# Row maxima of attention scores: one head's piece per bank, or whole banks that hold several heads

## The reference, cut to what matters

```python
qkv = clip(einsum('bsd,ed->bse', xn, Wqkv), -8, 8)
q, k = layer_norm(q), layer_norm(k)            # with weights and biases
scores = einsum('bqhd,bkhd->bhqk', q, k) * 16**-0.5 + slopes * (k_pos - q_pos)
scores = where(k_pos <= q_pos, scores, -1e30)
out = einsum('bhqk,bkhd->bqhd', softmax(scores), v) @ Wout.T
x + out * silu(ffn(xn))
```

## Time and profile before

| | us |
|---|---|
| median of 3 runs (lowest, highest) | 1176.12 (1174.08, 1177.57) |
| profiled execution, its own time | 1172.21 |
| its span, first to last instruction | 1170.4 |
| PE busy in the span | 1090.4 (93%) |
| DVE busy | 905.7 (77%) |
| ACT busy | 632.1 (54%) |
| POOL busy | 374.2 (32%) |

### The profile page before, as it was taken

One profiled execution on the slowest core, in us unless ns is written; L12 is line 12 of the kernel. 1 busy time (PEld: TensorE's weight loads), 2 busy tenths in 40 slices (PEclk: granted clock), 3 DMA queues, 4 the chain that ended last, 5 costly groups with the idle time before them and its releaser, 6 DMA issues. The chain is left out here.

```text
span 1170.4 us, 23869 instructions
## 1 busy us (share of the span) xinstructions
PE 1090.4 (93%) x6401; PEld 679.4 (58%) x6401; DVE 905.7 (77%) x2115; ACT 632.1 (54%) x956; POOL 374.2 (32%) x472
## 2 busy tenths in 40 slices
PE   6999996999999999999999998899999999999996
PEld 4778771333333333333333433688788878887885
DVE  6888888788788888878888883677857876777776
ACT  3333330666667667666667667644544464445443
POOL 2666662121221212121221212134523443443343
PEclk9999995999999999999999999999999999999999
DMA  6335373334543434344443522100110020012000
GB/s 239 111 106 159 114 196 93 119 116 103 149 105 90 134 89 129 90 125 103 124 120 91 132 73 85 37 1 10 55 45 0 18 90 0 0 36 73 1 1 37
DMA packets 99725, 99.34 MB, mean 85 GB/s; under 512 B 28144, under 2 KB 80992, under 8 KB 99552
## 3 DMA queue, kind: packets, MB, share of 16 engines
q1 hardware_dynamic: 73216, 85.82, 25.4%
q10 hardware_dynamic: 26464, 12.98, 3.7%
HBM read 77.13 MB, written 21.23 MB: 84 GB/s over the span
## 5 line engine op out<-in xcount | busy, mean ns | idle before, releaser
L878 ACT ACTIVATE pr<-pair 128x1024 f32<-128x1024 f32 (+3 forms) x384 | 292.1, 811 | 157.9 <-PE pair L1001 101.4
L273 DVE CUSTOM_DVE_ANT_0 bank<-bank,sg 128x384 f32<-128x384 f32 (+3 forms) x512 | 241.5, 515 | 74.8 <-PE bank L283 70.4
L1281 DVE SCALAR_TENSOR_TENSOR gate<-pair,sgu,gate 128x512 f32<-128x512 f32 x168 | 126.1, 751 | 95.3 <-PE pair L1365 95.2
L1364 PE MATMUL pair<-xc_lo,w_gu 128*128 128x512 f32 x448 | 175.6, 392 | 1.8 <-DVE xc_lo L1264 1.8
L1365 PE MATMUL pair<-xc_hi,w_gu 128*128 128x512 f32 x448 | 174.8, 390 | 0.0
L276 DVE TENSOR_REDUCE mx<-bank 128x1 f32<-128x512 f32 x256 | 159.8, 682 | 7.4 <-PE bank L283 6.7
L1135 POOL TENSOR_TENSOR h_lo<-gate,h_hi 128x512 fp32r<-128x512 f32 x56 | 72.5, 1294 | 245.4 <-ACT h_hi L1160 245.4
L283 PE MATMUL bank<-xin_c,s_sb 108*128 108x512 bf16 (+3 forms) x384 | 116.7, 349 | 13.1 <-DVE mx L273 10.2
L1195 ACT ACTIVATE gate<-gate 128x512 f32<-128x512 f32 x56 | 35.5, 634 | 169.6 <-DVE gate L1281 169.6
L283 PE MATMUL bank<-ks,qs 108*128 108x512 bf16 (+3 forms) x384 | 109.0, 330 | 7.9 <-DVE mx L273 6.9
L996 PE MATMUL pair<-s_sb,xin_c 111*128 111x512 bf16 (+3 forms) x384 | 94.6, 330 | 8.8 <-DMA s_sb<-dt 4.1
(11 more groups left out here) (111 smaller groups left out, 1968.4 us busy)
## 6 DMA issues: line engine op xcount, KB each, us to landing
stk<-parts ACTq DMA_DIRECT2D x16, 768.0 KB, 5.0
zst<-in_z_all SPq DMA_DIRECT2D x24, 448.0 KB, 4.2
xin_c<-in_x SPq DMA_DIRECT2D x32, 256.0 KB, 2.7
sst<-in_w_all SPq DMA_DIRECT2D x16, 448.0 KB, 5.1
s_sb<-stk SPq DMA_DIRECT2D x96, 64.0 KB
xin_c<-stk SPq DMA_DIRECT2D x96, 64.0 KB
qs<-stk SPq DMA_DIRECT2D x96, 64.0 KB
ks<-stk SPq DMA_DIRECT2D x96, 64.0 KB
```

The source lines that it names most:

```text
L273: dve.tensor_tensor_reduce(out=src, in0=src, in1=tri[:, 512 - w:512], scale=1.0, scalar=-3.0e38, op0=ALU.add, op1=ALU.max, accum_out=dst). ...
L878: act.activation(pr[e % 3][:, 2 * p:2 * p + 2, 0:w], pair[p][:, :, 0:w], ACT.Exp, scale=SCALE)\
L1281: dve.scalar_tensor_tensor(out=a, in0=GB[j % 4], scalar=scale_of(n, k, it), in1=a, op0=ALU.mult, op1=ALU.add)\
L1364: pe.matmul(GB[j % 4], w, xc_lo[:, k, :], start=True, stop=False)
```

## The change

1. **Pieces of whole banks.** The diagonal block of a query tile is a piece of its own: all 4 heads, 128 keys each, in one bank. The keys left of the diagonal are cut at 512; a remainder of 128 keys takes 4 heads to a bank, one of 256 keys 2 heads, one of 384 keys 1. A group has 38 pieces (27 early, 11 late) in place of 48 (32 and 16), with 72 score matmuls in place of 48.
2. **Masks by matmul.** Into each of the 8 diagonal banks a first matmul (`behind` against the identity, repeated 4 times, 512 columns) writes the mask; the four score matmuls add to it. `take` is then always one `tensor_reduce` with one maximum per head of the bank. `tri` goes.
3. **Negation on VectorE.** `negate` replaces `over_halves`: a `tensor_reduce` with `negate=True` over the parts of each maximum (2 for tiles 0 to 3, 3 for tiles 4 to 7; the tiles are set to -3e38 once), twice a group. GpSimd's `chain` loses its first operation, 4 are left. The wait of VectorE for `d_chain` moves from the first piece of each kind to `negate`.
4. **D0 counts two turns** of the ring (`D0_TURNS`), so that the ring's length is divisible by 3: the piece behind `D0` waits until the piece ahead of `D0` is taken.
5. **Spread by number.** Places are weighted by how long TensorE's steps last (`steps_of`), and every piece counts one. `HEAD`, `TAIL` and `BEFORE` go from 8, 6, 4 to 5, 3, 2.
6. Small tiles (maxima, negated maxima, `behind`) move into `sg0`; `behind` is loaded once, in the first block in place of `tri`, no longer on SyncE's queue at the start of the second.

```diff
-        tri = sg0
-        mx0 = sb("mx0", [P, GH, 4], F32)
-        mx1 = sb("mx1", [P, 2, GH, 4], F32)
+        mx0 = sg0[:, 0:32].rearrange("p (a t j) -> p a t j", a=2, t=4)
+        mx1 = sg0[:, 32:80].rearrange("p (a t j) -> p a t j", a=3, t=4)
+        dneg0, dneg1 = sg0[:, 80:96], sg0[:, 96:112]
+        behind = sg0[:, 128:192].bitcast(BF16)
...
+        def pieces(qt):
+
+            out = [(qt, qt * P, P, 0, GH)]
+            for k0 in range(0, qt * P, 512):
+                w = min(512, qt * P - k0)
+                n = 1 if w > 256 else 512 // w
+                out += [(qt, k0, w, j0, n) for j0 in range(0, GH, n)]
+            return out
...
+        EARLY = sorted(sum((pieces(qt) for qt in range(4, 8)), []), key=lambda pc: pc[1] == 0)
+        LATE = sum((pieces(qt) for qt in range(4)), [])
+        HEAD = 5
+        LATER_KEYS = sum(pc[1] > 0 for pc in EARLY)
...
-        TAIL = 6
-        BEFORE = 4
+        TAIL = 3
+        BEFORE = 2
+        D0_TURNS = 2
...
-            width = [w for e in range(NSTEP) for w in (512 - STEPS[e][2], 512 - STEPS[e][2], 512 - STEPS[e - 1][2])]
-            total, work = sum(width[lo:hi]), sum(pc[3] + 60 for pc in lot)
+            def steps_of(e):
+
+                w = 512 - STEPS[e][2]
+                second_w, pv_w = 2 * w + (2 * P if diag[e] else 0), 4 * w + 384
+                return second_w, pv_w
+            width = [w for e in range(NSTEP) for w in (steps_of(e)[0], steps_of(e)[0], steps_of(e - 1)[1])]
...
-                while at < len(lot) and (h == hi - 1 or sum(pc[3] + 60 for pc in lot[:at]) < work * passed / total):
+                while at < len(lot) and at * total < len(lot) * passed:
...
-        RING = len(order)
+        RING = len(order) - 1 + D0_TURNS
...
+            dve.tensor_reduce(dst, b[:, 0:heads * w].rearrange("p (j c) -> p j c", c=w), AX.X, ALU.max).then_inc(m_free, 1)
...
+            mask = k0 == qt * P
+            if mask:
+
+                pe.matmul(b[:, :], behind, identb[:, :].unsqueeze(1).to_broadcast([P, GH, P]), start=True, stop=False)
+            for j in range(heads):
+                mm = pe.matmul(b[:, j * w:(j + 1) * w], qs[s][0:ROWS_MAX, qt // 4, j0 + j, (qt % 4) * P:(qt % 4 + 1) * P],
+                               ks[s][0:ROWS_MAX, j0 + j, k0:k0 + w], start=not mask, stop=not mask or j == heads - 1)
...
-        def over_halves(dve, n):
+        def negate(dve, n, mx, dneg, done):
 
             dve.wait_ge(m_free, n)
-            dve.tensor_tensor(mx1[:, 0, :, :], mx1[:, 0, :, :], mx1[:, 1, :, :], ALU.max).then_inc(mx1_done, 1)
+            dve.tensor_reduce(dneg.rearrange("p (j t) -> p j t", j=GH), mx.rearrange("p c t j -> p j t c"),
+                              AX.X, ALU.max, negate=True).then_inc(done, 1)
```

More of the change, by code:

```diff
@@ L193, in load @@
                   .then_inc(stk_in[s][b], 16)
-        m_full, m_free, mx1_done, tri_done = sem("m_full"), sem("m_free"), sem("mx1_done"), sem("tri_done")
+        m_full, m_free, mx_set = sem("m_full"), sem("m_free"), sem("mx_set")
+        neg0_done, neg1_done, behind_in_sb = sem("neg0_done"), sem("neg1_done"), sem("behind_in_sb")
         b_m, b_o = bank[0:3], bank[3]
@@ L203, in build, with columns @@
         diag = [kt >= 4 * qb for qb, kt, _ in STEPS]
[L206 to L216, removed]
+        def pieces(qt):
[5 more added lines that the diff above has]
+            return out
+        def columns(pc):
+            return pc[2] * pc[4] * (2 if pc[1] == pc[0] * P else 1)
+        EARLY = sorted(sum((pieces(qt) for qt in range(4, 8)), []), key=lambda pc: pc[1] == 0)
+        LATE = sum((pieces(qt) for qt in range(4)), [])
+        HEAD = 5
+        LATER_KEYS = sum(pc[1] > 0 for pc in EARLY)
         PLACES = 3 * NSTEP
@@ L250, in build, with numbered @@
         PREP = len(HEAD_ORDER)
-        number = ({x: n for n, x in enumerate(order)}, {x: n for n, x in enumerate(own)})
+        def numbered(work):
+            return {x: n + (D0_TURNS - 1 if "D0" in work[:n] else 0) for n, x in enumerate(work)}
+        number = (numbered(order), numbered(own))
         def at(x, last):
@@ L359, in body @@
                         if first and u == 1:
-                            sp.dma_start(tri[:, :], tri_in).then_inc(tri_done, 16)
+                            sp.dma_start(behind, behind_in).then_inc(behind_in_sb, 16)
                             sp.dma_start(raw_out[:, :, :], wproj[:, :, 3 * D:].rearrange("k p c -> p k c"))\
@@ L645, in _ @@
                     take(dve, EARLY[n], b_m[n % 3], n)
[L646 removed]
+                negate(dve, len(EARLY), mx1, dneg1, neg1_done)
             @block.tensor
@@ L939, in ring @@
                         elif x in LATE[HEAD:] or not last:
-                            if x == EARLY[0]:
-                                dve.wait_ge(d_chain, 10 * i + 1)
-                            if x == LATE[0]:
-                                dve.wait_ge(d_chain, 10 * i + 6)
                             take(dve, x, ring_bank(x, last), base(i) + at(x, last))
                             if x == EARLY[-1]:
-                                over_halves(dve, base(i) + at(x, last) + 1)
+                                dve.wait_ge(d_chain, 2 * CH * i + CH)
+                                negate(dve, base(i) + at(x, last) + 1, mx1, dneg1, neg1_done)
+                            if x == LATE[-1]:
+                                dve.wait_ge(d_chain, 2 * CH * i + CH)
+                                negate(dve, base(i) + at(x, last) + 1, mx0, dneg0, neg0_done)
                 dve.memset(b_o[:, :], 0.0).then_inc(o_clear, 1)
@@ L1000, in second @@
                         for jj in range(2):
-                            mm = pe.matmul(pair[p][:, jj, 0:P], identb[:, :], behind[:, :], start=False, stop=True)
+                            mm = pe.matmul(pair[p][:, jj, 0:P], identb[:, :], behind, start=False, stop=True)
                     mm.then_inc(s_full[p], 1)
```

70 lines of the change are left out of this document (29 added, 41 removed).

## The result

| | before | after |
|---|---|---|
| median (lowest, highest), us | 1175.68 (1174.08, 1177.57), 4 runs | **1188.7** (1186.53, 1189.56), 4 runs |
| profiled execution's span, us | 1170.4 | 1184.6 |
| PE / DVE busy, us | 1090.4 / 905.7 | 1106.5 / 872.9 |

The ratio is 1.0107, 95% interval 1.0086 to 1.0129: slower by 13 us, almost four times what a measurement can tell from no change. The forecast was 1177.9 (no change); the range, up to 1190, holds the time.

The account below looks back on a forecast made before the run. The prediction took TensorE in the attention loop (busy 93.57 of 100 us) as the bound. Its terms summed to +0.12 us a group, x 15 = +1.8 us on a median of 1176.1, giving 1177.9 us; the range was 1166 to 1190.

Parts of the forecast that it names:

- steps 1 and 2: Attention group: one bank for five small pieces in step 2, -0.49 us; narrower late pieces of query tile 3, -0.16.
- step 3: Attention group: TensorE's work there gives 3.23 us in place of 3.31, -0.08 a group, bounds -0.4 and +0.3.
- steps 4 and 5: Attention group, ahead of D0's turn: no change expected, 0; step 5 keeps the same 512-wide pieces.
- step 6, D0's double turn: Attention group: the next piece's matmul starts 0.5 us late, until VectorE begins D0's copy; taken as +0.40, bounds 0 and 0.85.
- steps 7 and 8: Attention group: same 512-wide pieces; one moves from step 8 to step 7, +0.21 and -0.21 us, together 0.
- steps 9 and 10: Attention group: a 0.055 us matmul ahead of a `pv` becomes a 0.43 us bank, twice, with no wait to absorb it: +0.75.
- step 11: Attention group's end: two banks (0.75 us) replace four pieces with a wait for a bank (1.05 us): -0.30.
- the reading of step 2: Five small pieces' 1.45 us come from handing three banks to and fro; rival, TensorE's issue: 1192 us, chance 0.07.
- the rival with 1200 us: Packed banks: weight loads don't hide, scores cost 0.096 us in place of 0.055, 22 us in all; chance 0.06.
- The rival's threshold of 0.51: Slower rival on D0's double turn, chance 0.18: decides from a D0 term of 0.51 us, where the sum passes 0.23 a group.
- The edges: First block's end and `negate`, GpSimd and queue changes: `negate` and queues at nothing, both edges together 0, bounds -2 and +2 us.
- D0 at VectorE's bound: Steps 6 to 9: D0's wait paid on TensorE and again by VectorE, term 0.85 us a group, 1184.7 us; chance 0.18.

Follow-up runs that it names:

- mask_twice: The changed kernel with each mask matmul issued a second time into the same bank: 1210.39 us, ratio 1.0304.
- o0_turn: The changed kernel with D0 counting one turn of the ring and the normalising entry O0 at the group's end two: 1183.78 us, ratio 1.0076.
- pad48: The changed kernel with an unused tile of 48 floats a partition, putting the first block's tiles back at their addresses before the change: 1180.52 us, ratio 1.0050.
- before_pad16: The kernel before with one unused tile of 16 floats (64 bytes a partition) ahead of `mx0`: 1181.7 us, ratio 1.0067.
- pad48_o0_turn: The changed kernel with the edits of both pad48 and o0_turn: 1175.11 us, ratio 1.0003.
- merged: pad48_o0_turn with one bank moved behind the last `pv` and step 10's packed bank moved behind D1's transpose: 1163.65 us, ratio 0.9907.
- pad16: The changed kernel with an unused tile of 16 floats, so that the projections' tiles start 128 past a multiple of 256 bytes: 1184.41 us, ratio 1.0088.
- align_xin_only: The changed kernel padded so that among the projections' tiles only `xin` starts at a multiple of 256 bytes, `parts` and `vst` 64 past: 1188.51 us, ratio 1.0127.

## Why the prediction was right and wrong

By its own steps, in us per group:

| step of the prediction | forecast | measured |
|---|---|---|
| steps 1 and 2: one bank for five pieces; narrower pieces | -0.65 | -0.63 |
| step 3 | -0.08 | +0.08 |
| steps 4 and 5 | 0 | +0.02 |
| step 6, D0's double turn | +0.40 | +0.55 |
| steps 7 and 8 | 0 | +0.02 |
| steps 9 and 10 | +0.75 | +0.75 |
| step 11 | -0.30 | -0.28 |
| sum | +0.12 | +0.51 |
| outside the sum, in the whole loop: three odd groups wait for D1's DMA | 0 | +1.5 us |
| outside the sum, in the whole loop: group 0 grew by less than the others | 0 | -0.4 us |
| outside the loop: the projections | 0 | +5.1 us |

- **Right**: the reading of step 2 (the ring's hand-overs, not TensorE's issue), the packed scores at 0.055 to 0.056 apart, eight in a row (so the loads do hide in a row as short as that, and the rival with 1200 us is dead), packed maxima at 0.60, and steps 9 to 11. mask_twice shows the path that the sum assumed.
- **D0, mis-sized.** "I take +0.40, as some 0.1 of idle lies ahead of the next `pv`". The wait was 0.56 and all of it was paid: o0_turn takes 0.55 out of step 6, and no idle was left to absorb the 0.1. The signalling, taken as 0.05, was 0.14. The rival's threshold of 0.51 was passed, but its mechanism (a second payment on VectorE, term 0.85) did not come: step 8 is shorter by what step 7 is longer.
- **Step 3, a mixed base.** The 3.31 came from ScalarE's exponentials, the 3.23 from TensorE's own work. By TensorE's starts the step was 3.20 before and is 3.28 after. A difference wants the same event at both ends.
- **The edges: the step that failed.** "I take 0 for both edges together, bounds -2 and +2". The end of the first block came out inside these bounds (the head is 1.1 us shorter). But the sixth part of the change, the small tiles moved into another, was priced as instructions and a queue entry only, and never as what it does to the tiles behind it. It costs 5.1 us in the projections, in code that no line of the diff touches, and 6 to 8 us in all by pad48 and before_pad16.

So the forecast missed by 10.8 us. The loop's two mis-sized terms are (0.15 + 0.16) x 15 = 4.7 of it; the projections' 5.1 are the larger part; the rest, about 1, is smaller than the scatter of the runs. The range held it because its upper end had been set by another mechanism (D0 at VectorE's bound), which is luck in part: of the two causes behind the number, only one was in it.

## What to carry to other kernels

A diff that adds, drops or resizes a tile also moves all tiles allocated behind it: count the new starts, and where a DMA that fills the engines reads them in pieces of some 512 bytes, keep them at multiples of 256 (64 and 128 past one were both slow here). Take the starts from the built program: a count from the first tile leaves out what lies ahead of it. When unchanged code gets slower, compare its transfers' time from issue to landing before anything else. And where a bank must be issued somewhere, look for a place at which TensorE already waits for another engine's short operation; here two banks moved into such places were worth 11.5 us (pad48_o0_turn against merged).

## What the runs showed of the hardware

- The start of a tile in a partition alone changed the time of this kernel by 0.6%: 64 unused bytes cost 6.4 us (before_pad16), 192 give back 8 (pad48). With `parts` at 64 or at 128 past a multiple of 256 (after and five others, pad16) the stores of 768 KB take 4.5 and 6.6 us in turn where they take 4.0 and 5.6 at a multiple, and all DMA engines together move 279 to 295 GB/s in place of 347 (after, before). Durations of engine instructions on the same tiles did not change (the projection matmuls L687 and their like are 389 to 393 ns in the median).
- The queue that was slowed (ScalarE's stores) is not the one that is waited for (SyncE's load of x): VectorE's wait for x doubled, 5.6 to 10.4 us (after), and moving x's own tile did nothing (10.5, align_xin_only).
- One `tensor_reduce` with four outputs over 512 columns takes as long as one with a single output: 686 and 683 ns (after).
